# Sixth batch's shared parts held for the final sums; the second routing stage's leading batch gated, chosen and ranked inside the last attention period

## What is computed

```python
def ffn(x):                      # x: 8192 tokens x 256, layer-normed
    scores = softmax(x @ gate_w.T)                    # 16 experts in 4 groups
    keep the 2 groups whose two best scores sum highest; idx = top 2 experts in them
    y = sum over the 2 experts: weight * ((silu(x@We1+be1) * (x@We3+be3)) @ We2 + be2)
    z = (silu(x @ ws1 + bs1) * (x @ ws3 + bs3)) @ ws2 + bs2      # the shared expert
    return y + z
def attn(x):                     # linear attention, 16 heads of 16
    q, k, v = x @ w_qkv.T;  q, k = relu(q), relu(k)
    z = 1 / (sum(k) . q + eps);  out = ((v k^T) q) * z
    return out @ w_proj.T + b_proj
x = x + 0.5 * ffn(norm(x));  x = x + attn(norm(x));  x = x + 0.5 * ffn(norm(x))
```

## Time and profile before

| what | value |
|---|---|
| median of 3 runs | 1258.98 us (1256.32 to 1259.11) |
| profiled execution, its own time | 1257.57 us |
| its span in the profile | 1255.8 us |
| mean granted TensorE clock | 0.981 |
| TensorE matmuls busy | 1144.1 us (91%) |
| VectorE busy | 862.7 us (69%) |
| ScalarE busy | 761.7 us (61%) |
| GpSimd busy | 697.5 us (56%) |

### The profile page before, as it was taken

One profiled execution on the slowest core, in us unless ns is written; L12 is line 12 of the kernel. 1 busy time (PEld: TensorE's weight loads), 2 busy tenths in 40 slices (PEclk: granted clock), 3 DMA queues, 4 the chain that ended last, 5 costly groups with the idle time before them and its releaser, 6 DMA issues.

```text
span 1255.8 us, 26365 instructions
## 1 busy us (share of the span) xinstructions
PE 1144.1 (91%) x6696; PEld 900.3 (72%) x6696; DVE 862.7 (69%) x2774; ACT 761.7 (61%) x1698; POOL 697.5 (56%) x850
## 2 busy tenths in 40 slices
PE   7998999899999967899999999899999999999981
PEld 4554555899999946777877878455567999999750
DVE  6788874566666655668878687668734666676497
ACT  4445441688888835665656654444314888888497
POOL 3577776488888854000421403356752888887820
PEclk9999999999999998999999999999999999999996
DMA  9822237566555532102320300112286565555398
GB/s 357 296 94 94 98 107 199 169 174 173 171 171 158 154 115 88 35 33 67 115 89 28 109 18 34 35 68 85 102 268 210 169 171 172 171 165 157 106 395 361
DMA packets 93928, 181.53 MB, mean 145 GB/s; under 512 B 17592, under 2 KB 60368, under 8 KB 91990
## 3 DMA queue, kind: packets, MB, share of 16 engines
q1 hardware_dynamic: 66342, 110.44, 28.7%
q0 software_dynamic: 26016, 67.55, 15.5%
q10 hardware_dynamic: 1424, 1.86, 0.5%
HBM read 97.63 MB, written 86.08 MB: 146 GB/s over the span
## 4 chain that ended last, share of the span: by engine, by line
PE 61%; DVE 16%; ACT 10%; issue 5%; DMA 4%; POOL 3%; SPq 1%; DVEq 0%; ACTq 0%; POOLq 0%
PE bank L685 20%; PE bank L695 10%; PE bank L544 8%; PE bank L560 6%; PE bank L676 5%; PE bank L791 3%; PE bank L741 2%; DVE stat L1143 2%; ACT rows L1003 2%; POOL expert_rows L1674 2%; PE bank L717 2%; ACT rows L883 2%; ACT xn L1021 1%; PE bank L506 1%; DMA w<-routed_rows 1%
## 5 line engine op out<-in xcount | busy, mean ns | idle before, releaser
L1737 POOL DMA_INDIRECT routed_rows<-xn,rdest x286 | 282.6, 988 | 114.9 <-DVE rdest L1426 53.1
L685 PE MATMUL bank<-rows,att 128*128 128x128 f32 x2288 | 302.4, 275 | 0.5 <-ACT att L992 0.5
L685 PEld LDWEIGHTS bank<-rows,att 128*128 128x128 f32 x2288 | 278.3, 192 | 1.2 <-ACT att L992 1.0
L1674 POOL DMA_INDIRECT expert_rows<-rows,slots x160 | 155.2, 970 | 89.4 <-issue 55.6
L992 ACT COPY att<-w 128x512 f32 x286 | 177.0, 619 | 10.8 <-issue 4.7
L1443 DVE SCALAR_TENSOR_TENSOR rows<-bank,tile_b,att 128x128 f32<-128x128 f32 x286 | 100.3, 351 | 115.1 <-ACT att L997 107.1
L695 PE MATMUL bank<-w,rows 128*128 x572 | 170.8, 381 | 1.6 <-DVE rows L1443 1.5
L991 ACT COPY rows<-bank 128x256 f32<-128x256 f32 x286 | 106.6, 373 | 84.6 <-PE bank L676 82.3
L1456 DVE TENSOR_TENSOR xn<-bank,be 128x256 f32<-128x256 f32 x286 | 121.5, 425 | 30.8 <-issue 8.4
L907 ACT ACTIVATE silu<-bank,bs 128x512 f32<-128x512 f32 x64 | 43.9, 686 | 141.0 <-PE bank L544 140.9
L560 PE MATMUL bank<-ws,be 128*128 128x256 f32 x512 | 121.4, 386 | 7.4 <-DVE be L1346 7.3
(11 more groups left out here) (209 smaller groups left out, 2034.3 us busy)
## 6 DMA issues: line engine op xcount, KB each, us to landing
rows<-expert_rows SPq DMA_DIRECT2D x286, 129.5 KB
rows<-routed_rows SPq DMA_DIRECT2D x32, 512.0 KB, 4.0
w<-routed_rows SPq DMA_DIRECT2D x10, 1024.0 KB, 12.4
w<-in_w SPq DMA_DIRECT2D x2, 4096.0 KB, 19.7
out<-xres SPq DMA_DIRECT2D x16, 512.0 KB, 10.7
xres<-in_x SPq DMA_DIRECT2D x7, 1024.0 KB, 9.7
rows<-routed_rows SPq DMA_DIRECT2D x6, 1024.0 KB, 8.8
expert_rows<-pad SPq DMA_DIRECT2D x47, 129.5 KB, 6.6
```

The lines of the kernel that those rows point to most:

```text
L685: last = nc.tensor.matmul(rh_ps[t % RB][:, n * P:(n + 1) * P], m.rw13[:, t % RB, c * C + n * INTER:c * C + (n + 1) * INTER], m.rT[:, t % R ...
L1674: nc.gpsimd.indirect_dma_start(out=d.xg, out_offset=bass.IndirectOffsetOnAxis(ap=m.slots[:, slots_of(r), k, i:i + 1], axis=0), in_=m.xs[bu ...
L1737: nc.gpsimd.indirect_dma_start(out=d.yt, out_offset=bass.IndirectOffsetOnAxis(ap=m.rdest[:, n:n + 1], axis=0), in_=m.ry[:, n, :], in_offse ...
```

## The change

Batch 11 gets a name, `NEXT`, and joins the early ones: `fresh_in` and `ahead` make period 7 of attention transpose, gate and choose it, `rank(NEXT)` and `meta(NEXT)` stand behind the attention loop, and the routing loop only places it (`slots`) and scatters it. Its own turn in `route(1)` keeps two shared parts, 0 and 1, with the transposes of batch 12. All six shared parts of batch 13 (the sixth batch: 29, 31 to 34, 36) move from `TAIL[1]` to `HELD[1]`, where the final sums take five before piece 0 and one before each later piece. Because the held batch's transposed rows lie in `xn` during the experts, `ry` leaves `xn`: seven buffers, three in `rows`, four in `silu`. The core of the diff:

```diff
@@ -226,10 +227,12 @@
-    m.ry = m.xn
     m.table = m.att[0:1, NT * ROW:NT * ROW + 2 * TQ].bitcast(I32)
     m.gT = m.work.rearrange("p (g m n) -> p g m n", g=2, m=2)
     m.silu = sb("silu", [P, 2, HALF])
+    rest = SLOTS * ROW + RB * C + RB * P
+    m.ry = [m.rows[:, rest + n * C:rest + (n + 1) * C] for n in range(3)] + [
+        m.silu[:, n // 2, n % 2 * C:(n % 2 + 1) * C] for n in range(4)]
...
@@ -241,17 +244,17 @@
-FIRST = ((0, 5, 9, 14, 18, 23, 27, 32, 37), (0, 5, 9, 14, 18, 23))
-HELD = ((44, 46, 48), (35, *range(37, PARTS)))
+FIRST = ((0, 5, 9, 14, 18, 23, 27, 32, 37), (0, 2, 7, 11, 16, 20))
+HELD = ((44, 46, 48), (29, *range(31, PARTS)))
 TAIL = tuple(tuple(n for n in range(FIRST[L][-1], PARTS) if n not in HELD[L]) for L in range(LAYERS))
-UPS, DOWNS = (4 * 7 + 2, 4 * 14), (PAIRS * 7 + 2, PAIRS * 14)
-HELD_UP, HELD_DOWN = ((7, 2), (14, 0)), ((7, 1), (14, 0))
-BIASED = (7, 6, 0, 1, 2, 3, 4, 5)
+UPS, DOWNS = (4 * 7 + 2, 4 * 13), (PAIRS * 7 + 2, PAIRS * 13)
+HELD_UP, HELD_DOWN = ((7, 2), (13, 0)), ((7, 1), (13, 0))
+BIASED = (7, 6, 5, 0, 1, 2, 3, 4)
 
 
 def held_ahead(n):
 
-    return HELD[1][n + 3 if n else 0:n + 4]
+    return HELD[1][n + 4 if n else 0:n + 5]
...
@@ -283,6 +286,18 @@
+
+
+NEXT = BATCHES + EARLY
+
+
+def fresh_in(b):
+
+    return NEXT if b == BATCHES - 1 else early_in(b, 0)
+
+
+def ahead(r):
+    return BATCHES <= r <= NEXT
...
@@ -616,27 +631,25 @@
                         if more and j % 2 == 0:
                             transpose(r + 1, j // 2)
 
-                    def turn_and_first_half(j):
-                        turn(j)
-                        first_half(j)
-
                     def second_half(j):
                         if more and j % 2 == 0:
                             transpose(r + 1, 2 + j // 2)
 
                     n, end = FIRST[L][b - LEAD[L]:b - LEAD[L] + 2]
-                    if b == LEAD[L]:
-                        if L:
-                            shared(L, n, turn_and_first_half)
-                            shared(L, n + 1, second_half)
-                        else:
-                            gate(r)
-                            shared(L, n, turn)
-                            shared(L, n + 1)
-                            shared(L, n + 2, first_half)
-                            shared(L, n + 3, second_half)
+                    if r == NEXT:
+                        shared(L, n, first_half)
+                        shared(L, n + 1, second_half)
+                        for j in range(n + 2, end):
+                            shared(L, j)
+                        continue
+                    if r == 0:
+                        gate(r)
+                        shared(L, n, turn)
+                        shared(L, n + 1)
+                        shared(L, n + 2, first_half)
+                        shared(L, n + 3, second_half)
                         rank(r)
-                        for j in range(n + (2 if L else 4), end):
+                        for j in range(n + 4, end):
                             shared(L, j)
...
@@ -852,16 +865,13 @@
                         a_transpose(b + 1, p)
-                    else:
-                        transpose(BATCHES + EARLY, p)
                 if more:
                     keys(b + 1, 0)
                     keys(b + 1, 1)
                 if ranked is not None:
                     rank(ranked)
                 outputs(b, PAIRS - 1)
-                if not more:
-                    gate(BATCHES + EARLY)
+            rank(NEXT)
...
@@ -904,6 +914,9 @@
                 act.wait_ge(s.h1_ready, 4 * (L * BATCHES + b) + u + 1)
+                if (L * BATCHES + b, u) in HELD_UP:
+                    for t in range(TILES * (L + 1) - RYSLOTS, TILES * (L + 1) - 3):
+                        act.wait_ge(s.rows_out[t % SLOTS], 16 * (t // SLOTS) + 16)
                 nc.scalar.activation(m.silu[:, mi, :], h1_ps[mi][:], ACT.Silu,
...
@@ -937,16 +950,15 @@
                         continue
-                    if b == LEAD[L]:
-                        normalise(r + 1)
-                        exponentials(r)
+                    if r == NEXT:
+                        normalise(r + 1, range(PAIRS))
                         copy_xT(r + 1, 0)
+                        normalise(r + 1, range(PAIRS, NT))
                         shared(L, n)
                         copy_xT(r + 1, 1)
                         copy_xT(r + 1, 2)
                         shared(L, n + 1)
                         copy_xT(r + 1, 3)
-                        meta(r)
                         for j in range(n + 2, end):
...
@@ -1227,9 +1239,12 @@
                     next(ahead_stats)
+                if r in (0, NEXT + 1):
                     for _ in range(5):
                         next(chosen)
                         yield
+                if r == NEXT + 1:
+                    negate_mean(r + 1)
                 yield from ahead_stats
...
@@ -1372,28 +1387,27 @@
                     r = L * BATCHES + b
-                    work = route_work(r)
+                    work = iter(()) if r == NEXT else route_work(r)
                     n, end = FIRST[L][b - LEAD[L]:b - LEAD[L] + 2]
                     if r == 0:
                         shared(0, n, work, 6)
                         shared(0, n + 1, work, 6)
                         for _ in work:
                             pass
-                    elif b == LEAD[L]:
-                        for _ in work:
+                        for _ in slots(r):
+                            pass
+                        for j in range(n + 2, end):
+                            shared(L, j, iter(()), 0)
+                        continue
+                    if r == NEXT:
+                        for _ in slots(r):
                             pass
                         shared(L, n, iter(()), 0)
                         shared(L, n + 1, iter(()), 0)
-                    if b == LEAD[L]:
-                        for _ in slots(r):
+                        for _ in stats_work(r + 2):
                             pass
-                        if L:
-                            for _ in stats_work(r + 2):
-                                pass
                         for j in range(n + 2, end):
                             shared(L, j, iter(()), 0)
-                        if L:
-                            negate_mean(r + 2)
                         continue
...
@@ -1580,8 +1595,6 @@
                     combine(b + 1, 1)
-                else:
-                    route_stats(BATCHES + EARLY)
...
@@ -1592,8 +1605,7 @@
                 else:
-                    negate_mean(BATCHES + EARLY)
-                    route_stats(BATCHES + EARLY + 1)
+                    route_stats(NEXT + 1)
                 sum_keys(b, 1)
...
@@ -1614,13 +1626,16 @@
                     route_stats(following)
                 if fresh is not None:
-                    steps(work, 2)
+                    steps(work, 2 if more else 5)
                 add(b, 2)
                 if fresh is not None:
+                    steps(work, 2 if more else 5)
+                add(b, 3)
+                if fresh is not None and more:
                     steps(work, 2)
-                add(b, 3)
-                if fresh is not None:
-                    steps(work, 2)
+                if not more:
+                    for _ in work:
+                        pass
                 if ranked is not None:
...
@@ -1695,8 +1710,6 @@
                     send(r, j // NT, j % NT)
-                    if b == BATCHES - 1 and j == 3:
-                        rstd(BATCHES + EARLY)
                     if b == BATCHES - 1 and j == NT - 1:
...
@@ -1804,8 +1817,8 @@
                     a_rstd(b + 1)
-                if early_in(b + 1, 0) is not None:
-                    rstd(early_in(b + 1, 0))
+                if b + 1 < BATCHES and fresh_in(b + 1) is not None:
+                    rstd(fresh_in(b + 1))
```

46 lines of the change are left out of this document (24 added, 22 removed).

## The result

The changed kernel takes 1268.43 us (median, 1267.88 to 1270.41), the kernel before in the same job 1257.8: a ratio of 1.0095, 95% interval [1.0079, 1.0111]. By that ratio it is slower by 0.95%, 12 us; the two medians lie 10.6 us apart. Its profiled execution took 1268.95 us, with a span of 1267.2 against 1255.8: 11.4 us to explain. The prediction said 1268.2.

What follows compares the result with a forecast made beforehand. A different engine bounds each stage's end, so four places were priced: experts' start +2.5, clock +2.7 and final sums +4.7 gave +9.9 us, taken as 1268.2 us, range 1256 to 1275.

Steps and rivals of the forecast that it cites:

- Period 7 and part 0: End of attention: `sel` of batch 11 at 805.1, part 0 starting at 805.8 instead of 797.40, 8.4 us later.
- Parts 0 and 1, and the clock: Start of routing: batch 12's transposes wait about 1.7 and 1.5 us; parts done at 817.7, gate of batch 12 at 818.7.
- rival C: Worse: two 6 us routing waits each drop the clock, 1.9 us each, and the reload takes 19.1: 1274; chance 0.10.
- Part 2: Routing stage: VectorE makes batch 13's statistics first, so TensorE's turn waits 2.1 us; the part ends at 824.6.
- Part 3 lets GpSimd through: Routing stage: GpSimd's delayed `rstd` of batch 13 ends at 833.2, so TensorE waits 6.5 us for that batch's transposes.
- From there to part 28: Later routing: from 849, the 85.4 us left before plus 6.9 for two more parts, so part 28 ends at 941.3.
- Reload and start: Start of experts: reload takes 17 us, weights at 958.3, first transposes 959.2 against 956.71, +2.5 us.
- Clock after the idle time: Start of experts: after TensorE's idle time it runs at half clock for 5.4 us, losing 2.7 us (bounds 0 and 4).
- Final sums: End of kernel: piece 0 weighed 4.4 us late, three more `silu`, less 1.4 idle: +4.7 us (bounds 1.5 and 6).
- Costed at nothing: Seven `ry` buffers, ScalarE's scatter waits ahead of held `silu`, bias order: 0; about 1 us per layer's end if cover fails.
- A: Routing stage keeps its pace: part 28 through at 933, experts 5.7 us earlier, +1.7 in all, 1260.0; chance 0.19.
- B: Faster: part 28 ends before about 930, -7.8 us, 1250.5; against it, scatters landing late beside the reload; chance 0.15.

Runs made afterwards that it cites:

- Experiment 4: Changed kernel with GpSimd's two waits inside the scatter of batch 11 set to parts 1 and 3 instead of 3 and 6: 1262.64 us, ratio 1.0044.
- experiment 3: Changed kernel with the reload of w2 and w13 cut into pieces issued behind parts 10, 16, 22 and 28: 1257.32 us, ratio 0.9993.
- experiment 12: Changed kernel with 56 unread matmuls added on TensorE ahead of the experts; they ran behind the idle time, not in it: 1295.13 us, ratio 1.0286.
- experiments 1: Kernel before with only the held parts (29, 31 to 34, 36) moved behind the experts, batch 11's routing as before: 1256.64 us, ratio 1.0006.
- experiment 10: Kernel before with held parts moved, cut-up reload mostly ahead of padding writes, be2 loaded earlier, four held parts before piece 0, two before piece 1: 1254.68 us, ratio 0.9975.
- experiments 7: Kernel before with the held parts moved behind the experts and the reload cut up, batch 11's routing outside attention: 1253.15 us, ratio 0.998.
- 9: Kernel before with held parts moved and the reload cut up, all but its last quarter of w13 ahead of the padding writes: 1250.11 us, ratio 0.9936.
- experiment 8: Changed kernel with batch 12's mean first, GpSimd released early, the reload cut up and be2 asked for behind the third expert rows: 1251.24 us, ratio 0.9953.
- 11: Changed kernel with batch 12's mean first, early GpSimd release, cut-up reload mostly ahead of padding writes, early be2, four held parts before piece 0: 1256.12 us, ratio 0.9979.

## Why the prediction was right

The direction, the places and most of the mechanism came out, and the sum (+9.9 for 11.4 on the spans) is close. Its three terms were off by +5.3, -1.8 and -2.0, which partly cancel. That the total came within 0.3 us (1268.2 for 1268.43) is luck: it leans on figures of the kernel before of 1257.57 and 1258.98, whose median with one execution more is 1257.8.

- *Period 7 and part 0.* `sel` at 805.13 (said: 805.1), part 0 at 806.12 (805.8). Given the up to 5 us by which whole profiles are shifted, some of that agreement is luck; the wait of 5.71 for "about 6" is not.
- *Parts 0 and 1, and the clock.* The agreement up to the gate of batch 13 (850.95 for 849) hides two errors that cancel. The waits inside parts 0, 1 and 5, put at 1.7, 1.5 and 1.3, were 0.47, 0.37 and nothing. And the forecast left out the half clock behind the two long waits, which cost 2.5 and 3.1 us; the prediction had it only in rival C.
- *Part 2.* Turn wait 1.75 (2.1). *Part 3 lets GpSimd through*: `rstd` ends at 833.89 (833.2), TensorE waits 6.56 (6.5). Experiment 4 shows it as the cause of half of this wait; the other half is the place of the mean in VectorE's order, which would hold TensorE for 3.48 us even with an early `rstd`.
- *From there to part 28.* Here the step failed in size: the reload is issued at 946.27 and not at 941.3. The gate of batch 13 is 2.0 later than 849. The "same is left as before and two parts more" left out that `rstd` of batch 14 is late too (855.73, queued behind the wait for part 6): VectorE gets its mean at 857.44 and falls behind, TensorE stands 3.55 us for `sel` of batch 13, and the passes behind this wait take 1.6 us longer at the half clock. From this gate to the reload TensorE's waits come to 6.45 us, where the kernel before has 4.75 from its gate at 844.95 on: 1.7 and 1.6 are about the other 3.0. The late `rstd` was in the text, its consequence was not. Experiment 4 gives 5.5 us of the reload's time back and shrinks this wait to 1.50.
- *Reload and start.* Issue to first transposes 18.2 us (17.9 said). That the reload is the bound is shown by experiment 3. This term came to +7.8, predicted +2.5.
- *Clock after the idle time.* The clock was 0.50 as said, for about 4 us and not for 5.4, and the cost is 0.9 us against the kernel before and 1.3 against experiment 12, not 2.7. While it was low ScalarE's copies set part of the pace, which the lower bound had allowed for. By the rule of the Trainium skill cited in the prediction (TensorE: Matmul & The Clock Gate, "Why this matters for your kernels") the restart is slow; the trace agrees, and in experiment 3 the clock is 1.00 where the gap is gone.
- *Final sums.* Piece 0 is weighed 4.3 us late (said: 4.4), measured from the first held part. But ScalarE's stretch from there to its end shrank from 57.2 to 55.8: it lost 2.7 us of idle time, not 1.4, and took three more `silu` (1.7 us). So +2.7, not +4.7.
- *Costed at nothing.* True in the changed kernel: ScalarE stands 4.95 us for the scatters ahead of its first held `silu`, but its second one starts 5.4 us behind the first held part in both kernels. Where the experts start earlier, the wait for `be2` appears (1.3 and 1.7 us of TensorE in experiments 1 and 3); taking it away in experiment 10 saved nothing, for TensorE then waits 1.7 us for rows.

The rivals. A didn't come. Half of C did: the clock fell behind both of its waits, at 2.5 and 3.1 us and not 1.9 each, and behind the one at 872. Its other half, a reload of 19.1 us, didn't: the second load landed 17.2 us behind its issue. B's collision is real: experiments 7 and 9 show that what runs beside the last sends delays their landing, 13.3, 9.5 and 4.6 us. The prediction cited the Trainium skill for it (DMA: Bandwidth & Descriptors, "Queues, rings and completion order"). The three distances agree with that rule. They would also agree with a mere sharing of the DMA engines, since no run here looked at a single DMA engine.

What stays open: whether the choice of batch 11 inside attention can pay. With its waits mended (experiment 8) the kernel is at 0.9953 [0.9936, 0.997], without it (experiment 9) at 0.9936 [0.9921, 0.995], and the two differ in more than this. Where they are made alike (experiments 10 and 11) it is 0.9975 and 0.9979, so no gain was seen. The wait for `sel` of batch 11 itself (5.9 us in experiments 8 and 11) was never mended.
